# The turned x kept once in fp32: one store and one load in place of a high and a low half, with the halves made again in the attention

## The reference, cut to what matters

```python
xn  = layernorm(x)
att = softmax(mask(q @ kwin.T / sqrt(512))) @ vwin @ Wout + bout   # q, k, v = xn @ Wqkv + bqkv; own block and its two neighbours
h   = bitlinear(xn, w_fc) + gate * (xn @ v.T @ fast_b.T @ u.T)
ffn = bitlinear(relu(h) ** 2, w_proj)
out = x + att + ffn
```

## The kernel before

| step | before |
|---|---|
| c = 0 | two blocks of xT_lo for tile i + 1 |
| c = 1 | two blocks of xT_hi for tile i + 2 |
| c = 2 and c = 3, each | one store of the output, one load of the feed-forward result |

## Time and profile before

### The profile page before, as it was taken

How to read it: one execution, slowest core, us unless ns; L and a number is a source line. 1 busy time by engine, 2 the same in 40 slices (tenths; PEclk the granted TensorE clock), 3 DMA queues, 4 the chain that set the end, 5 groups by cost and what they waited for, 6 DMA issues and landing times.

```text
span 2400.5 us, 56237 instructions
## 1 busy us (share of the span) xinstructions
PE 2341.3 (98%) x19528; PEld 1912.8 (80%) x19528; DVE 1675.9 (70%) x4576; ACT 1374.2 (57%) x3488; POOL 441.6 (18%) x734
## 2 busy tenths in 40 slices
PE   6999999999999999998999999999999999999997
PEld 5888888888888888886788888888887888888885
DVE  6455544555545444535888888888888888988896
ACT  6333333333333333324777777777777777777775
POOL 2011111111111001102222222222222222222222
PEclk8999999999999999999999999999999999999999
DMA  5643344433344444314899999999999999999996
GB/s 188 206 113 110 102 114 122 117 102 109 110 122 122 114 113 122 105 36 133 261 293 296 292 296 291 290 300 283 298 289 294 293 292 288 294 291 290 291 286 191
DMA packets 390109, 495.74 MB, mean 207 GB/s; under 512 B 35792, under 2 KB 296400, under 8 KB 389888
## 3 DMA queue, kind: packets, MB, share of 16 engines
q1 hardware_dynamic: 389744, 492.71, 69.7%
q0 software_dynamic: 144, 0.17, 0.0%
HBM read 261.53 MB, written 231.21 MB: 205 GB/s over the span
## 4 chain that ended last, share of the span: by engine, by line
PE 27%; DMA 9%; ACT 7%; issue 4%; DVE 4%; SPq 2%; POOL 0%; POOLq 0%; DVEq 0%
PE job_ps L1353 8%; PE job_ps L1362 5%; PE job_ps L1513 5%; ACT wqkv_raw L1134 5%; PE score_ps L1440 4%; DMA turned_pairs<-pair_blocks 4%; DMA pair_moved<-turned_pairs 3%; PE job_ps L1371 3%; DVE wqkv_raw L1212 2%; PE pT_ps L1456 2%; SPq L1035 1%; DMA turned_blocks<-wqkv_raw 1%; ACT pT L1143 1%; DMA wqkv_raw<-turned_blocks 1%; ACT q_hi L1159 1%
## 5 line engine op out<-in xcount | busy, mean ns | idle before, releaser
L1134 ACT ACTIVATE wqkv_raw<-wqkv_raw,neg_max 128x384 f32<-128x384 f32 (+1 forms) x1024 | 619.3, 606 | 218.8 <-DVE neg_max L1212 215.8
L643 ACT ACTIVATE relu<-up_ps,fc_scale 128x512 f32<-128x512 f32 x256 | 176.1, 688 | 633.5 <-PE up_ps L753 633.5
L704 DVE SCALAR_TENSOR_TENSOR sq<-up_ps,relu 128x512 f32<-128x512 f32 x256 | 177.0, 692 | 494.5 <-ACT relu L643 493.3
L1212 DVE CUSTOM_DVE_ANT_0 wqkv_raw<-score_ps,mask 128x384 f32<-128x384 f32 (+1 forms) x1024 | 504.0, 549 | 25.1 <-PE score_ps L1440 24.2
L765 PE MATMUL down_ps<-proj_T,sq_lo 128*128 128x512 f32 x1024 | 404.7, 395 | 0.0
L763 PE MATMUL down_ps<-proj_T,sq_hi 128*128 128x512 f32 x1024 | 404.3, 395 | 0.2 <-DVE sq_lo L687 0.2
L749 PE MATMUL up_ps<-f_xT_hi,fc_T 128*128 128x512 f32 x1024 | 400.3, 391 | 2.2 <-PEq L136 2.2
L751 PE MATMUL up_ps<-f_xT_lo,fc_T 128*128 128x512 f32 x1024 | 400.3, 391 | 0.0
L1229 DVE STREAM_TRANSPOSE wqkv_raw<-wqkv_raw 128x384 f32<-128x384 f32 (+1 forms) x508 | 282.6, 573 | 66.9 <-ACT wqkv_raw L1134 64.2
L1353 PE MATMUL job_ps<-xT_hi,wqkv_hi 128*128 128x256 f32 x1024 | 309.9, 303 | 0.1
L1353 PE MATMUL job_ps<-xT_lo,wqkv_hi 128*128 128x256 f32 x1024 | 289.2, 282 | 0.0
(11 more groups left out here) (158 smaller groups left out, 4374.3 us busy)
## 6 DMA issues: line engine op xcount, KB each, us to landing
turned_blocks<-wqkv_raw SPq DMA_DIRECT2D x123, 768.0 KB, 4.8
wqkv_raw<-turned_blocks SPq DMA_DIRECT2D x492, 192.0 KB, 4.1
turned_pairs<-pair_blocks SPq DMA_DIRECT2D x124, 384.0 KB, 4.1
pair_moved<-turned_pairs SPq DMA_DIRECT2D x496, 96.0 KB, 3.3
xT_hi<-xT SPq DMA_DIRECT2D x65, 256.0 KB, 4.9
xT_lo<-xT SPq DMA_DIRECT2D x65, 256.0 KB, 5.0
xT<-f_xT_hi SPq DMA_DIRECT2D x64, 256.0 KB, 2.9
xT<-f_xT_lo SPq DMA_DIRECT2D x64, 256.0 KB, 3.1
```

The source lines that it names most:

```text
L643: nc.scalar.activation(relu[:, s % 2, :], up_ps[:, s % 2, :], ACT.Relu, scale=fc_scale2[:, s:s + 1]).then_inc(relu_done, 1)
L704: nc.vector.scalar_tensor_tensor(sq[:, s % 2, :], up_ps[:, s % 2, :], 0.0, relu[:, s % 2, :], ALU.max, ALU.mult).then_inc(sq_done, 1)
L1134: nc.scalar.activation(probs[:, u, cols], probs[:, u, cols], ACT.Exp, bias=neg_max[:, u:u + 1], scale=-1.0, accum_out=prob_sum[:, u:u + 1] ...
L1212: nc.vector.tensor_tensor_reduce(out=probs[:, u, cols], in0=score_ps[:, h, cols], in1=mask[:, cols], scale=-SCORE_SCALE, scalar=3e38, op0= ...
```

## The change

- In the feed-forward stage, the turned tile is stored from `x_in` in fp32, once: 4 stores of 256 KB for a tile in place of 8, issued once x_in is filled and no longer after the halves are made. The first tile, of four blocks, is stored as before, in halves, into a tensor of its own.
- `load_x` there waits in addition until the tile stored before has landed. For the second tile this is a wait for the eight stores of the first. ScalarE's copy to f_xT_hi loses its wait for older stores.
- In the attention, blocks 4 to 63 are loaded in fp32 into a new buffer, `x_staged`, of two blocks. ScalarE rounds them into `xT_hi` (two copies of 128 x 512 in c = 0 of tile j - 1, behind `qk_high`), and GpSimd subtracts to `xT_lo` (two subtractions of 128 x 256 in c = 0 and two in c = 1 of the same tile, between `copy_keys` and `widen_inverse_sums(t, 1)`). TensorE waits on `x_split`.
- The loads stand in c = 3 of tile i for tile i + 2, both blocks, 2 x 256 KB, ahead of that step's two other side transfers. The loads of c = 0 and of c = 1 are gone.

```diff
@@ feed_forward_stage, sync
             def load_x(i):
                 sp.wait_ge(xT_done, NB * i)
+                for b in range(NB):
+                    sp.wait_ge(xT_stored[b], 16 * i + 16)
                 settle(sp, ticks)
...
-            def store_xT(i, par):
+            def store_first_xT():
                 for b in range(NB):
-                    sp.wait_ge(xT_done, NB * (i + 1))
+                    sp.wait_ge(xT_done, NB)
                     settle(sp, ticks)
                     for low, xT in enumerate((xT_hi, xT_lo)):
-                        sp.dma_start(xT_rows(xT_dram, NB * i + b, low),
-                                     xT[:, par, :, b * P:(b + 1) * P].bitcast(F32)).then_inc(xT_stored[b], 16)
-            store_xT(0, 0)
+                        sp.dma_start(xT_rows(first_xT_dram, 2 * b + low),
+                                     xT[:, 0, :, b * P:(b + 1) * P].bitcast(F32)).then_inc(xT_stored[b], 16)
+            def store_xT(i):
+                sp.wait_ge(x_blocks_in, 16 * STRIPS * i)
+                settle(sp, ticks)
+                for b in range(NB):
+                    sp.dma_start(xT_rows(xT_dram, NB * i + b), x_in[:, :, b * P:(b + 1) * P]).then_inc(xT_stored[b], 16)
+            store_first_xT()
...
@@ attention_stage
+        x_staged = sb("x_staged", [P, 2, DC, P], F32)
+        def x_block(j, r):
+            return (2 * j + 1 + r) % NBLK
+        def staged_rows(j):
+            return [r for r in range(2) if j >= 0 and x_block(j, r) >= DC]
+        def staged_before(j):
+            return sum(len(staged_rows(m)) for m in range(j))
+        def slot_free(j):
+            return A_NUMBER[4 * (j - XR) + 5]
@@ sync
+            def load_x(j):
                 for r in range(1 if j < 0 else 0, 2):
+                    blk = x_block(j, r)
+                    if r in staged_rows(j):
+                        if j >= 2:
+                            sp.wait_ge(x_split, 2 * staged_before(j))
+                        sp.dma_start(x_staged[:, r, :, :], xT_rows(xT_dram, blk)).then_inc(x_staged_here, 16)
+                        continue
...
-                if c == 0 and 1 <= i < NT - XR + 2:
-                    load_x(i + XR - 2, 1)
-                if c == 1 and i + XR - 1 < NT:
-                    load_x(i + XR - 1, 0)
+                if c == 3 and i + XR - 1 < NT:
+                    load_x(i + XR - 1)
@@ gpsimd
+            def x_low(j, half):
+                rows = staged_rows(j)
+                if half == 0:
+                    pool.wait_ge(x_rounded, j)
+                cols = slice(half * DC // 2, (half + 1) * DC // 2)
+                for r in rows:
+                    nc.gpsimd.tensor_tensor(xT_lo[:, x_slot(j) + r, cols, :], x_staged[:, r, cols, :],
+                                            xT_hi[:, x_slot(j) + r, cols, :].bitcast(F32), ALU.subtract
+                                            ).then_inc(x_split, 1)
...
+                if where(t)[1] < 2 and where(t)[0] + 1 < NT:
+                    x_low(where(t)[0] + 1, where(t)[1])
@@ scalar
+            def round_x(j):
+                act.wait_ge(x_staged_here, 16 * staged_before(j + 1))
+                if j >= XR - 1:
+                    act.wait_ge(job_filled, slot_free(j))
+                for r in staged_rows(j):
+                    last = nc.scalar.copy(xT_hi[:, x_slot(j) + r, :, :], x_staged[:, r, :, :])
+                last.then_inc(x_rounded, 1)
...
+                if where(t)[1] == 0 and where(t)[0] + 1 < NT:
+                    round_x(where(t)[0] + 1)
@@ tensor, run_a
-                        pe.wait_ge(x_here[i % XR], 64 * (1 + i // XR) + (32 if i % XR == XR - 1 else 0))
+                        pe.wait_ge(x_split, 2 * staged_before(i + 1))
+                        if i in (1, NT - 1):
+                            pe.wait_ge(x_here[i % XR], 32 if i == 1 else 64)
```

More of the change, by code:

```diff
@@ L59, in load_dealt_rows, with xT_rows @@
         sp.dma_start(x_in[q * DH:(q + 1) * DH, b, :], x[bass.ds(tile * D + q * P + b * DH, DH), :]).then_inc(here, 16)
-def xT_rows(dram, block, low):
-    return dram[bass.ds((2 * block + low) * P, P), :].rearrange("p (k t) -> p k t", k=DC)
+def xT_rows(dram, block):
+    return dram[bass.ds(block * P, P), :].rearrange("p (k t) -> p k t", k=DC)
 def identity_on_pool(pool, nc, ident, zeroed, ready):
@@ L448, in _, with feed_forward_stage @@
                     nc.scalar.copy(low_out[:, g * D:(g + 1) * D], first_ps[0:3 * DH, (g + 1) % 2, :]).then_inc(u_copied, 1)
-def feed_forward_stage(nc, x, fast_b, w_fc, w_proj, u, v, gate, xT_dram, x_turned_dram, partial, weights):
+def feed_forward_stage(nc, x, fast_b, w_fc, w_proj, u, v, gate, xT_dram, first_xT_dram, x_turned_dram, partial, weights):
     F = w_fc.shape[0]
@@ L590, in tile @@
                 if not is_last(i):
-                    store_xT(i + 1, 1 - par)
+                    store_xT(i + 1)
             tiles(sp, tile)
@@ L598, in _ @@
                 sp.wait_ge(stored[b], 16 * (NT + 1))
-                sp.wait_ge(xT_stored[b], 32 * NT)
+                sp.wait_ge(xT_stored[b], 16 * NT + 16)
         @block.gpsimd
@@ L623, in xT_high @@
                 act.wait_ge(x_blocks_in, 16 * STRIPS * i)
-                for b in range(NB):
-                    wait(act, xT_stored[b], 32 * (i - 1))
                 nc.scalar.copy(xT_hi[:, par, c, :], x_in[:, c, :]).then_inc(xT_hi_done, 1)
@@ L781, in _, with attention_stage @@
                 down(NT - 1, s)
-def attention_stage(nc, loaded, xT_dram, partial, turned_dram, pair_dram, out):
+def attention_stage(nc, loaded, xT_dram, first_xT_dram, partial, turned_dram, pair_dram, out):
     NBLK = partial.shape[0] // P
@@ L847, in attention_stage @@
         x_here = [sem(f"xT_here{r}") for r in range(XR)]
+        x_staged_here, x_rounded, x_split = sem("x_staged_here"), sem("x_rounded"), sem("x_split")
         job_filled = sem("job_filled")
@@ L881, in x_slot @@
             return 2 * (i % XR)
-        def x_loads(i):
-            return i // XR + (2 if i % XR == XR - 1 else 1)
+        def x_block(j, r):
[6 more added lines that the diff above has]
+            return A_NUMBER[4 * (j - XR) + 5]
         def own_tokens(xT, i, k):
@@ L978, in _ @@
         def _(sp):
[L979 to L983, removed]
+            def load_x(j):
                 for r in range(1 if j < 0 else 0, 2):
-                    blk = (2 * j + 1 + r) % NBLK
-                    sp.dma_start(xT[:, x_slot(j) + r, :, :].bitcast(F32), xT_rows(xT_dram, blk, low)).then_inc(
-                        x_here[j % XR], 16)
+                    blk = x_block(j, r)
[5 more added lines that the diff above has]
+                    if j >= XR - 1:
+                        sp.wait_ge(job_filled, slot_free(j))
+                    for low, xT in enumerate((xT_hi, xT_lo)):
+                        sp.dma_start(xT[:, x_slot(j) + r, :, :].bitcast(F32), xT_rows(first_xT_dram, 2 * blk + low)
+                                     ).then_inc(x_here[j % XR], 16)
             def load_part(i, b):
@@ L1042, in _ @@
             for j in range(-1, XR - 1):
-                for low in range(2):
-                    load_x(j, low)
+                load_x(j)
             sp.wait_ge(wout_lo_done, 1)
@@ L1607, in feed_forward @@
 def feed_forward(nc, x, partial, fast_b, w_fc, w_proj, u, v, gate, out):
-    xT_dram = nc.dram_tensor("xT", [2 * x.shape[0], x.shape[1]], F32, kind="Internal").ap()
+    xT_dram = nc.dram_tensor("xT", [x.shape[0], x.shape[1]], F32, kind="Internal").ap()
+    first_xT_dram = nc.dram_tensor("first_xT", [2 * D, x.shape[1]], F32, kind="Internal").ap()
     x_turned_dram = nc.dram_tensor("x_turned_blocks", [P // DH, DC, P, D // DC], F32, kind="Internal").ap()
@@ L1624, in feed_forward @@
                                    (sem("wqkv_here"), sem("wout_here"), sem("biases_here")))
-        feed_forward_stage(nc, x, fast_b, w_fc, w_proj, u, v, gate, xT_dram, x_turned_dram, partial, weights)
-        attention_stage(nc, weights, xT_dram, partial, turned_dram, pair_dram, out)
+        feed_forward_stage(nc, x, fast_b, w_fc, w_proj, u, v, gate, xT_dram, first_xT_dram, x_turned_dram, partial, weights)
+        attention_stage(nc, weights, xT_dram, first_xT_dram, partial, turned_dram, pair_dram, out)
 _INS = ["L0_attn_x", "L0_attn_Wqkv", "L0_attn_bqkv", "L0_attn_Wout", "L0_attn_bout", "L0_ffn_fast_b", "L0_ffn_w_fc",
```

## The result

The changed kernel takes 2423.84 us (median of 6 runs, 2422.80 to 2427.39) against 2405.49 us for the kernel before (6 runs, 2403.74 to 2405.78). The ratio is 1.0085, with a 95% interval of 1.0072 to 1.0098: 18.4 us slower. The forecast was 2409.5 with a range of 2397 to 2422, "same" the likeliest. The time lies just outside it, at the place of the rival called crowding.

What follows compares the result with a forecast made beforehand. It took attention to be bound by TensorE's floor plus waits on a just-in-time DMA queue. Terms +3.2, +18.0, +3.0 and -20.4 gave +3.8 us, 2406.1 against the profiled run, 2409.5 as run median; range 2397 to 2422.

Steps and rivals of the forecast that it cites:

- crowding: Rival, chance 0.26, slower: four side transfers ahead of pair_out cost 1.0 us or more per step c = 0; 2421.5 to 2433.5.
- The bound: Attention: TensorE's floor of 9.74 and 9.80 us per step, plus 18.9 us of waits on a just-in-time DMA queue.
- the wait in c = 0: Attention, step fed by c = 3's four side transfers: TensorE waits 0.6 us, in 30 tiles, +18.0 us.
- delay 1.4: Attention queue: two more side transfers ahead of pair_out delay it and all behind it by 1.4 us, ends 1.2 and 1.8.
- margin 0.9: Attention: pair_in lands 0.9 us before TensorE needs it after a relieved step, in place of the usual 0.4.
- idle time of 0.3 to 0.8 us: Attention: DMA engines idle this long in quiet steps might absorb added transfers, so the c = 0 wait's lower end is 0.
- The other three steps: Attention, steps c = 1, 2, 3: waits shrink to about 0.1 us per tile together, +3.0 us over 30 tiles.
- The old waits: Attention: the earlier waits of 0.68 us per tile go, -20.4 us over 30 tiles.
- The feed-forward wait: Second feed-forward tile: loads wait for the first tile's stores, TensorE stands once, +3.2 us, ends 2.0 and 6.
- ScalarE's rounding: Attention, c = 0: two copies taking 1.14 us fit into ScalarE's 1.42 us gap, cost 0.
- GpSimd's subtractions: Attention, c = 0 and 1: 1.5 us per step fits into GpSimd's 2.48 us idle before rcp_wide, cost 0.
- Relief: Rival, chance 0.13, faster: the DMA queue drains with 4.5% less traffic; 2388.5 us, or 2397.5 with some waits left.

Runs made afterwards that it cites:

- e2: Changed kernel with four staging blocks in place of two, x loads in c = 0 and c = 1 instead of both in c = 3; 2396.16 us, ratio 0.9972.
- e3: Changed kernel with one load of x in c = 2 and one in c = 3, instead of both in c = 3; 2416.87 us, ratio 1.0054.
- e5: Kernel before, with only the two loads of xT_hi moved from c = 1 to c = 3, nothing staged, rounded or subtracted; 2432.62 us, ratio 1.0104.
- e7: Changed kernel with four staging blocks, x loads in c = 0 and c = 1, and no load_x wait in the second feed-forward tile; 2394.60 us, ratio 0.9953.

## Why the prediction was wrong

**The bound** was read rightly. TensorE has a floor of 9.74 and 9.80 us per step, the DMA queue delivers pair_in just in time, and the sum of waits is what a change can win or lose. In e2 the waits shrink to 5.8 us, with ScalarE's new work inside the step c = 0.

**The step that failed is the size of one term, the wait in c = 0: "I take delay 1.4 less margin 0.9 and 0.1 for scatter: 0.6".** It is 1.05 us. The delay was right for pair_out: that of c = 3 lands 5.6 us after its issue in the changed kernel and 4.2 in the kernel before (means of the 28 steps), 1.4 later, and pair_in is issued 5.24 us into c = 0 in place of 3.88. The margin of 0.9 was wrong, in two ways.

First, it was given to the wrong step. It is the margin of a pair_in that was sent with no side transfers, with the last of the earlier trace rows, and c = 3 stands two steps behind an empty one, with c = 2 and its two transfers between them. By then most of the room is gone: in c = 3 of the changed kernel, pair_in is issued at 3.44 us in place of 3.79, and blocks_out at 5.69 in place of 5.93.

Second, margins were read from one step, with the median landing of four transfers added to the last issue. Over the 28 steps of each kind they come out smaller. In a step without a wait TensorE starts the second part 8.97 us into the step (9.03 in c = 1 and 2), and where it waits, 0.14 us behind the last landing of pair_in. So landings up to 8.83 (8.89) cost nothing. Pair_in's last transfer lands, on the mean:

| TensorE's step | kernel before | margin | changed kernel | margin |
|---|---|---|---|---|
| c = 1 (sent in 0) | 8.94 | -0.05 | 8.55 | 0.34 |
| c = 2 (sent in 1) | 8.94 | -0.05 | 8.42 | 0.47 |
| c = 3 (sent in 2) | 8.72 | 0.11 | 8.53 | 0.30 |
| c = 0 (sent in 3) | 8.87 | -0.04 | 9.86 | -1.03 |

The usual margin was nothing, not 0.4, which is why every step of the kernel before had some wait. The margin ahead of c = 0 in the changed kernel was 0.30, not 0.9, and from there to the landing behind four transfers it is 1.33 us. So delay 1.33 less margin 0.30 gives 1.03, the wait of 1.05. (The delay of 1.4 less the prediction's usual 0.4 gives 1.0 as well, but by luck: against the kernel before pair_in lands only 1.0 later, not 1.4, as it lands faster after its issue, and the margin it meets is none.)

Lateness carries over, as e3 and e5 show; room hardly does, as the table and the 0.35 us of c = 3 in e3 show. The reason is argued and not tested: in both kernels blocks_out is never issued before 5.55 us into a step, when VectorE has turned its blocks, nor pair_out before 9.43, so a chain that runs ahead is held at these points. With 1.0 in its place the sum of the prediction is 15.8 us, and the measured loss 18.4. With this term and the two below as measured, it is 3.8 + 30 x 1.05 + 30 x 0.12 - 20.4 = 18.5.

**That the added work might fit into idle time of 0.3 to 0.8 us** of the DMA engines was the reason for a low end of 0. It was read from two single steps. Over the 28 steps c = 0 the mean share goes from 0.97 to 1.00, so about 0.3 us was taken up, and the wait is not smaller for it. In c = 1 and 2, where nothing was to be added, it falls from 0.99 and 1.01 to 0.82 and 0.93.

**The other three steps, 0.1 us per tile:** 0.12 measured (0.04 + 0.02 + 0.06). The old waits, 0.68 per tile, did go in these.

**The feed-forward wait, +3.2 with ends 2.0 and 6:** 3.8 in the changed kernel's profile, 1.7 to 2.6 in the four others with the wait, so mostly near or below the low end. The loads began 10.08 us after the first store in place of 7.05, 3.0 later, where I had 2.9. But the fifth of them began only 2.3 us later, as the first four were issued in 1.8 us in place of 2.5. TensorE's wait was seen in all five profiles, the fallen clock in one.

**ScalarE's rounding, 0:** right. In c = 0 of the changed kernel:

```profile
1407.16 1.14 ACT L1161 CAST xT_hi<-x_staged 128x512 fp32r<-128x512 f32 x2
...
1408.69 0.62 ACT L1176 ACTIVATE wqkv_raw<-wqkv_raw,neg_max 128x384 f32<-128x384 f32 x1 [0.39 <-DVE neg_max L1256]
```

The two copies take 1.14 us, and 0.39 us are still idle where 1.42 were the earlier trace rows. **GpSimd's subtractions, 0:** right, 0.72 us each, with 1.66 us idle before rcp_wide:

```profile
1408.38 1.43 POOL L1124 TENSOR_TENSOR xT_lo<-x_staged,xT_hi 128x256 fp32r<-128x256 f32 x2 [0.80 <-ACT xT_hi L1161]
1411.47 0.29 POOL L1108 COPY rcp_wide<-sum_rcp 128x128 f32<-128x128 f32 x1 [1.66 <-DVE sum_rcp L1265]
```

**The rivals.** Crowding is the case that came, at its price with 1.0 us of wait (2421.5 predicted), and by the sign that was named for it, steps c = 0 of over 10.7 us (10.79). Relief, the faster one, was no idle thought: in its weak form it was 8.2 us faster than the kernel before, and e2 is 6.7 and e7 11.3 us faster by the ratios, once the transfers are not bunched. I held against it that the change bunches them, rightly. The rule of the Trainium skill that went with it (DMA: Bandwidth & Descriptors, Latency and other measured facts: lighter load, smaller fixed cost) did not save the changed kernel. Its DMA share is 0.93 against 0.99, and pair_out of c = 3 lands later than before, after 5.6 us in place of 4.2; the queue ahead of it decides. Whether the fixed part shrank as well, no run here shows.

## What to carry to other kernels

Where a chain of dependent transfers runs through a queue that is nearly full, count the bytes ahead of the critical transfers in each step, and not the bytes of a period: half the traffic of x was saved and lost again because it was put into one step, and spreading it turned 0.85% slower into 0.28% faster (0.47% with the first wait gone too). Take a margin as the mean over many steps, from the last landing to the use, and in the same position as the step it is spent in, since room won two steps earlier may be gone while lateness is handed on. And a wait added for reuse of a buffer has to be looked at in the first iteration, where the long lead of the steady state does not exist.

## What the runs showed that was not expected

- Four transfers of 256 KB ahead of pair_out cost the kernel before more (e5, 26.6 us) than the changed kernel (18.4), with almost the same wait in c = 0 (1.14 and 1.05). Two more in the next step keep the lateness going, 0.37 us in c = 1 against 0.04, which is 9 of the 15 us by which the waits of the two differ.
- Putting the loads behind the critical pair_out made the step 0.9 us worse than putting them ahead of it (1.95 against 1.05), since they then stand ahead of blocks_in, in SyncE's issue order and in the queue.
- The preparation ahead of the first store scatters by 2.7 us between profiles of kernels that are the same up to there (52.57 to 55.31), as much as the feed-forward wait it stands next to costs; only a length between two events of one trace could tell them apart.
